# Layer norms between the layers: the inverse root on GpSimd by iteration in place of ScalarE's square root

## The reference

```
def _layernorm(x, axis=-1, eps=1e-05):
    m = jnp.mean(x, axis=axis, keepdims=True)
    v = jnp.var(x, axis=axis, keepdims=True)
    return (x - m) / jnp.sqrt(v + eps)
...
x = _layernorm(x + _L0_attn_ref(x, ...), axis=-1)   # 16 heads, polynomial attention (scores ** 4), causal
x = _layernorm(x + _L0_ffn_ref(x, ...), axis=-1)    # 2 experts, one chosen for each token
x = _layernorm(x + _L1_attn_ref(x, ...), axis=-1)   # 32 heads, softmax attention, causal
x = _layernorm(x + _L1_ffn_ref(x, ...), axis=-1)    # 32 experts, 6 chosen for each token, and a shared one
```

## Time and profile before

| | |
|---|---|
| device time, median of 3 runs | 1570.79 us (1561.16 to 1575.43) |
| span of the profiled execution, first to last instruction | 1555.2 us |
| mean granted clock of TensorE in it | 0.903 |
| instructions | 26255 |
| ACT_TABLE_LOADs | 31, 1283 ns each |
| norms | 16 |

### The profile page before, as it was taken

How to read it: one execution, slowest core, us unless ns; L and a number is a source line. 1 busy time by engine, 2 the same in 40 slices (tenths; PEclk the granted TensorE clock), 3 DMA queues, 4 the chain that set the end, 5 groups by cost and what they waited for, 6 DMA issues and landing times.

```text
span 1555.2 us, 26255 instructions
## 1 busy us (share of the span) xinstructions
PE 1299.0 (84%) x9336; PEld 836.8 (54%) x9336; DVE 1053.5 (68%) x2755; ACT 880.1 (57%) x1250; POOL 673.1 (43%) x834
## 2 busy tenths in 40 slices
PE   6377764776789999689999998889899879899995
PEld 5233352332567877444444554445444445799984
DVE  7767687868543355877888476776887465455675
ACT  2478725778443343337778566676667641466660
POOL 7477334648301103412332741222247626766761
PEclk9589985899899999759999989988889999999999
DMA  2591000012302100000000000000004434677886
GB/s 94 175 362 65 1 1 1 1 41 82 105 32 68 41 15 26 21 1 1 2 1 1 1 1 1 1 2 1 1 31 153 172 144 161 211 210 212 265 263 229
DMA packets 69079, 124.32 MB, mean 80 GB/s; under 512 B 7319, under 2 KB 55127, under 8 KB 67929
## 3 DMA queue, kind: packets, MB, share of 16 engines
q1 hardware_dynamic: 56664, 85.92, 17.2%
q0 software_dynamic: 12288, 36.72, 6.3%
HBM read 60.22 MB, written 62.39 MB: 79 GB/s over the span
## 4 chain that ended last, share of the span: by engine, by line
PE 52%; DVE 26%; ACT 11%; POOL 5%; issue 4%; DMA 2%; SPq 0%; POOLq 0%; DVEq 0%; ACTq 0%
PE psum L2380 9%; PE psum L2275 8%; PE psum L2576 6%; DVE psum L2967 6%; PE psum L2364 6%; PE psum L2475 5%; PE psum L2336 3%; ACT probs L2701 3%; DVE probs L2987 3%; PE psum L2599 3%; PE psum L2496 3%; DVE neg_max L2970 2%; PE psum L351 2%; ACT qt L2618 2%; PE psum L2296 2%
## 5 line engine op out<-in xcount | busy, mean ns | idle before, releaser
L2699 ACT ACTIVATE probs<-psum,exp_shift 128x1024 f32<-128x1024 f32 (+1 forms) x320 | 321.9, 1032 | 137.2 <-PE psum L2364 133.8
L2967 DVE CUSTOM_DVE_ANT_0 psum<-psum,stage 128x512 f32<-128x512 f32 (+3 forms) x512 | 287.1, 621 | 89.0 <-PE psum L2336 88.4
L3552 POOL TENSOR_SCALAR_AFFINE_SELECT probs<-probs 128x512 f32<-128x512 f32 x192 | 139.6, 739 | 410.5 <-ACT probs L2699 308.4
L2364 PE MATMUL psum<-qt,kt 32*128 32x512 f32 (+5 forms) x1152 | 243.4, 456 | 54.7 <-ACT probs L2701 19.4
L2336 PE MATMUL psum<-kt,qt 32*128 32x512 f32 (+3 forms) x768 | 228.8, 467 | 29.9 <-DVE neg_max L2967 21.3
L2364 PEld LDWEIGHTS psum<-qt,kt 32*128 32x128 f32 (+1 forms) x1152 | 108.0, 199 | 214.4 <-issue 84.3
L2987 DVE TENSOR_TENSOR probs<-probs 128x1024 f32<-128x1024 f32 (+1 forms) x136 | 169.6, 1291 | 62.3 <-ACT probs L2701 62.0
L2380 PE MATMUL psum<-probs,v 128*32 128x256 f32 (+3 forms) x2048 | 179.8, 450 | 1.9 <-POOL probs L3552 1.9
L3623 POOL DMA_INDIRECT results<-sp_y,sp_row x128 | 125.7, 982 | 57.2 <-ACT sp_y L2760 28.8
L2336 PEld LDWEIGHTS psum<-kt,qt 32*128 32x128 f32 x768 | 107.5, 204 | 69.7 <-DVE neg_max L2967 42.2
L2701 ACT ACTIVATE probs<-psum 128x1024 f32<-128x1024 f32 (+1 forms) x160 | 140.3, 947 | 5.7 <-PE psum L2364 5.6
(11 more groups left out here) (344 smaller groups left out, 2550.2 us busy)
## 6 DMA issues: line engine op xcount, KB each, us to landing
many_x<-blank SPq DMA_DIRECT2D x2, 10240.0 KB, 50.5
sp_xs<-many_x SPq DMA_DIRECT2D x64, 320.0 KB, 3.7
sp_w<-in_sparse SPq DMA_DIRECT2D x8, 1280.0 KB, 9.8
x_turned<-results SPq DMA_DIRECT2D x8, 768.0 KB, 6.4
sp_back<-results SPq DMA_DIRECT2D x8, 768.0 KB, 9.3
sorted_x<-blank SPq DMA_DIRECT2D x2, 1152.0 KB, 6.5
sorted_y<-y SPq DMA_DIRECT2D x18, 128.0 KB, 1.7
rows<-in_x SPq DMA_DIRECT2D x4, 512.0 KB, 6.8
```

Source lines behind the costliest of these rows:

```text
L2364: inst = pe.matmul(psum[:, base - early:base + QCH - q0], A.kt[rows, k_slot, key * P:(key + 1) * P], A.qt[rows, q_slot, c * QCH + q0 - ear ...
L2699: inst = act.activation(dst, view, ACT.Exp, bias=exp_shift[:, 0:1])
L2967: inst = dve.tensor_tensor_reduce(src, src, causal_bf[:, (4 - cols) * P:4 * P], -1.0, -MASKED, ALU.add, ALU.min, dst)
L3552: pool.affine_select(out=dst, in_=dst, compare_op=ALU.is_ge, fill=0.0, base=0, pattern=[[0, 4], [1, P]], channel_multiplier=-1).then_inc(p ...
```

## The change

The 10 norms that do not stand in the first attention or at the end of the last layer go another way to the inverse root; the other 6 keep the old one (`by_sqrt=True`). In the 10:

- DVE makes the statistics as before; L3023 now multiplies by a constant as well. One more `tensor_scalar` on DVE (`norm_newton`, `ln_rstd<-ln_sd`) makes a first guess of the inverse root: it takes the bits of the number as an integer, halves them and subtracts them from a constant. It stands where `root` stands.
- POOL refines the guess in ten operations on 128x4 numbers, each of which waits for the one before, and then `norm_scale` on POOL runs the four `tensor_scalar` of 128x256 on x.
- ACT has no part in these norms; DVE has no reciprocal and no scaling.
- PE and SP have the same instructions in the same order as before.

```
--- before.py
+++ after.py
@@ -23,6 +23,10 @@
 BANK = 512
 QCH = 512
 EPS = 1e-5
+ROOT_STEPS = ("product", "square", "less", "first", "product 2", "square 2", "less 2", "times 2", "plus 2", "root")
+FIRST_ROOT = 0x5F1FFFF9
+ROOT_A, ROOT_B = 0.703952253, 2.38924456
+ROOT_SCALE = (0.375 * ROOT_A) ** -2
 WEIGHTS_AHEAD = 2
 MANY, WIDTH, SHARED = 32, 96, 192
 GATED = 2 * WIDTH
...
@@ -527,16 +532,23 @@
                     mark(normed, *names[0])
                     mark(normed, *names[1])
                     mark(normed, *names[2])
-                    do("norm_moments", g=g, names=names, ready=ready)
+                    do("norm_moments", g=g, names=names, ready=ready, by_sqrt=by_sqrt)
 
                 def root():
-                    mark(rooted, *names[2])
-                    do("norm_root", g=g, names=names)
+                    if by_sqrt:
+                        mark(rooted, *names[2])
+                        do("norm_root", g=g, names=names)
+                        return
+                    mark(normed, *names[2], "guess")
+                    for what in ROOT_STEPS:
+                        mark(pool_normed, *names[2], what)
+                    do("norm_newton", g=g, names=names)
 
                 def scale():
-                    mark(normed, *names[3])
-                    x_ready[g] = (mark(normed, *names[4]),)
-                    do("norm_scale", g=g, names=names)
+                    if by_sqrt:
+                        mark(normed, *names[3])
+                    x_ready[g] = (mark(normed if by_sqrt else pool_normed, *names[4]),)
+                    do("norm_scale", g=g, names=names, by_sqrt=by_sqrt)
 
                 return [moments, root, scale]
 
@@ -593,7 +605,7 @@
                 norms_due = []
 
                 def norm():
-                    for part in plan_norm(norms_due.pop(0)):
+                    for part in plan_norm(norms_due.pop(0), True):
                         part()
 
                 def x_to_channels(b, c, free):
...
@@ -3008,7 +3020,7 @@
                 dve.tensor_tensor(xs, pair_of_banks(slot).rearrange("p (t n) -> p t n", t=4), xs, ALU.add
                                   ).then_inc(added.by(A.layer, g), 1)
 
-            def norm_moments(g, names, ready):
+            def norm_moments(g, names, ready, by_sqrt):
                 t0, t1 = 4 * g, 4 * g + 4
                 for e in ready:
                     q.wait_ge(*e)
@@ -3020,10 +3032,22 @@
                     inst = dve.bn_aggr(ln_mean_var[:, t, :], ln_stats[:, t, :])
                 inst.then_inc(normed.by(*names[1]), 1)
                 q.wait_ge(normed, *names[1])
-                dve.tensor_scalar(ln_sd[:, t0:t1], ln_mean_var[:, t0:t1, 1], EPS, None, ALU.add
-                                  ).then_inc(normed.by(*names[2]), 1)
-
-            def norm_scale(g, names):
+                if by_sqrt:
+                    dve.tensor_scalar(ln_sd[:, t0:t1], ln_mean_var[:, t0:t1, 1], EPS, None, ALU.add
+                                      ).then_inc(normed.by(*names[2]), 1)
+                else:
+                    dve.tensor_scalar(ln_sd[:, t0:t1], ln_mean_var[:, t0:t1, 1], ROOT_SCALE, ROOT_SCALE * EPS, ALU.mult, ALU.add
+                                      ).then_inc(normed.by(*names[2]), 1)
+
+            def norm_newton(g, names):
+                t0, t1 = 4 * g, 4 * g + 4
+                q.wait_ge(normed, *names[2])
+                dve.tensor_scalar(ln_rstd[:, t0:t1].bitcast(mybir.dt.int32), ln_sd[:, t0:t1].bitcast(mybir.dt.int32),
+                                  -0.5, float(FIRST_ROOT), ALU.mult, ALU.add).then_inc(normed.by(*names[2], "guess"), 1)
+
+            def norm_scale(g, names, by_sqrt):
+                if not by_sqrt:
+                    return
                 t0, t1 = 4 * g, 4 * g + 4
                 q.wait_ge(rooted, *names[2])
                 dve.reciprocal(ln_rstd[:, t0:t1], ln_sd[:, t0:t1]).then_inc(normed.by(*names[3]), 1)
@@ -3544,6 +3568,41 @@
                 pool.tensor_tensor(at_lo, nm, at.bitcast(F32), ALU.subtract).then_inc(pool_cut.by("max", b, g, half), 1)
                 q.wait_ge(pool_cut, "max", b, g, half)
 
+            def norm_newton(g, names):
+                t0, t1 = 4 * g, 4 * g + 4
+                v, y, r, s = ln_sd[:, t0:t1], ln_rstd[:, t0:t1], ln_stats[:, t0:t1, 0], ln_stats[:, t0:t1, 1]
+
+                q.wait_ge(normed, *names[2], "guess")
+                pool.tensor_tensor(r, v, y, ALU.mult).then_inc(pool_normed.by(*names[2], "product"), 1)
+                q.wait_ge(pool_normed, *names[2], "product")
+                pool.tensor_tensor(r, r, y, ALU.mult).then_inc(pool_normed.by(*names[2], "square"), 1)
+                q.wait_ge(pool_normed, *names[2], "square")
+                pool.tensor_scalar(s, r, -1.0, ROOT_B, ALU.mult, ALU.add).then_inc(pool_normed.by(*names[2], "less"), 1)
+                q.wait_ge(pool_normed, *names[2], "less")
+                pool.tensor_tensor(y, s, y, ALU.mult).then_inc(pool_normed.by(*names[2], "first"), 1)
+                q.wait_ge(pool_normed, *names[2], "first")
+                pool.tensor_tensor(r, v, y, ALU.mult).then_inc(pool_normed.by(*names[2], "product 2"), 1)
+                q.wait_ge(pool_normed, *names[2], "product 2")
+                pool.tensor_tensor(r, r, y, ALU.mult).then_inc(pool_normed.by(*names[2], "square 2"), 1)
+                q.wait_ge(pool_normed, *names[2], "square 2")
+                pool.tensor_scalar(s, r, ROOT_A ** 4, -10 / 3 * ROOT_A ** 2, ALU.mult, ALU.add).then_inc(pool_normed.by(*names[2], "less 2"), 1)
+                q.wait_ge(pool_normed, *names[2], "less 2")
+                pool.tensor_tensor(s, s, r, ALU.mult).then_inc(pool_normed.by(*names[2], "times 2"), 1)
+                q.wait_ge(pool_normed, *names[2], "times 2")
+                pool.tensor_scalar(s, s, 5.0, None, ALU.add).then_inc(pool_normed.by(*names[2], "plus 2"), 1)
+                q.wait_ge(pool_normed, *names[2], "plus 2")
+                pool.tensor_tensor(y, s, y, ALU.mult).then_inc(pool_normed.by(*names[2], "root"), 1)
+                q.wait_ge(pool_normed, *names[2], "root")
+
+            def norm_scale(g, names, by_sqrt):
+                if by_sqrt:
+                    return
+                t0, t1 = 4 * g, 4 * g + 4
+                for t in range(t0, t1):
+                    inst = pool.tensor_scalar(x[:, t, :], x[:, t, :], ln_mean_var[:, t, 0:1], ln_rstd[:, t:t + 1],
+                                              ALU.subtract, ALU.mult)
+                inst.then_inc(pool_normed.by(*names[4]), 1)
+
             def mask_weights(A, b, quad, c, step, p_slot, ready):
                 for e in ready:
                     q.wait_ge(*e)
...
```

More of the change, by code:

```diff
@@ L471, in build_program @@
         pool_raised = signal("pool_raised", "POOL")
+        pool_normed = signal("pool_normed", "POOL")
         ident_in, later_in = loading("ident"), loading("later")
@@ L519, in plan_half_to_channels, with plan_norm @@
                 return done
-            def plan_norm(g):
+            def plan_norm(g, by_sqrt=False):
                 names = [("ln", g, next(norm_count), i) for i in range(5)]
@@ L2048, in finish @@
                 def finish(c):
-                    for part in plan_norm(c):
+                    for part in plan_norm(c, True):
                         part()
@@ L2073, in plan_sparse @@
                     if (t, third) == (4, 0):
-                        moments, root, scale = plan_norm(0)
+                        moments, root, scale = plan_norm(0, True)
                         moments()
@@ L3415, in _ @@
                      scores=scores, normalize=normalize, project_out=project_out, norm_moments=norm_moments,
-                     norm_scale=norm_scale, many_setup=many_setup, piece_low=piece_low,
+                     norm_newton=norm_newton, norm_scale=norm_scale, many_setup=many_setup, piece_low=piece_low,
                      sort_by_token=sort_by_token, sort_choose=sort_choose, sort_rank=sort_rank, turn_group=turn_group,
@@ L3627, in _ @@
             walk(dict(attention_setup=attention_setup, bias_setup=bias_setup, project=project, head_scale=head_scale, cut=cut,
[L3628 removed]
+                     cut_max=cut_max, norm_newton=norm_newton, norm_scale=norm_scale, mask_weights=mask_weights, sorted_setup=sorted_setup,
                      piece_low=piece_low, scatter=scatter, gather=gather, many_setup=many_setup,
```

1 line of the change is left out of this document (removed).

## The result

The changed kernel took 1582.74 us (median of 4 runs, 1570.58 to 1593.32) beside 1565.97 us (4 runs, 1561.05 to 1575.43) for the kernel before: a ratio of 1.0119 with a 95% interval of 1.0076 to 1.0161. It is slower by 1.2%. Measured twice more beside experiments, it stood at 1.0115 (1.0075 to 1.0154) and 1.0134 (1.0082 to 1.0185). The forecast was 1569.7 us, within 1% of the kernel before, in a range of 1556 to 1580; the measured time lies above that range.

The account below looks back on a forecast made before the run. No engine is full; PE, busy 84% and half the chain, is bound by its waits around norms. Terms -0.5, 0, +1.7, +6.6, +0.9, -7.6 sum to +1.1 us gained: span 1554.1, plus 15.6 gives 1569.7 us, range 1556 to 1580.

Parts of the forecast that it names:

- 1. norms 2, 3, first expert layer: First expert layer: POOL idle, scaled rows ready at 441.0 and 456.0, PE's turns at 441.49 and 455.00; -0.5 us.
- 3. start of the second attention: Second attention's start: DVE's scaling goes and most of PE's 1.92 us wait with it; +1.7 us (0 to 1.9).
- 4. chunks 0 and 1: Second attention: DVE's maxima no longer held back, 4.65 us, plus 2.0 of clock; +6.6 us (2 to 9.6).
- 5. chunk 2: Second attention: half of PE's 1.83 us wait behind ACT goes, POOL's 5.8 fit before its next mask; +0.9 us.
- 6. chunk 3: Seam to the last layer: norm waits behind POOL's scatters, rows at 1288.7 in place of 1281.11; -7.6 us.
- the clock at chunk 0: Behind PE's wait at chunk 0: granted clock, 0.60 before, rises above 0.9; 1.6 us to be had there.
- the step spacing: POOL's ten dependent operations on 128x4: 0.30 us apart, 3.0 us in all; 2.4 if the overhead guess is too high.
- the table loads: ACT: sixteen table loads of 1.283 us go, 31 become 15, 20.5 us taken from ACT.
- the queue of six scatters at chunk 3: POOL at chunk 3: guess ready at 1279.4, but six scatters stand ahead, the last until 1282.9.
- POOL's scaling: Four scalings of 128x256 on POOL: 0.71 us each, 2.8 together; over 1 us each would show the forecast wrong.
- B: Slower rival: POOL's queue binds at the seam, second attention doesn't pass gains on; 8.9 us lost, 1579.7 us; chance 0.25.
- C: Rival: scaling x on POOL slows DVE where both read SBUF; 2 to 5 us lost; chance 0.05.

Follow-up runs that it names:

- e8: Changed kernel, four subtract-then-multiply scalings of a norm given different operands, constant or for each partition; doesn't compute the layers; ran once, 1592.02 us.
- e10: Changed kernel with other scaling forms on POOL (multiply-then-add with operands for each partition or constants, subtract alone); doesn't compute the layers; ran once, 1637.67 us.
- e11: Changed kernel with POOL's scaling as multiply-then-add and two more small steps, at all ten norms; 1.0065 of the kernel before.
- e1: Changed kernel with the norms of chunks 2 and 3 back on ACT's root and DVE's scaling; 0.9967, repeated 0.9994 of the kernel before.
- e2: Changed kernel with norms 2 and 3 of the first expert layer back on ACT's root and DVE's scaling; 1.0018, repeated 1.0033 of the kernel before.
- e3: Changed kernel with first expert layer's norms 2, 3 and second attention's chunks 2, 3 back on ACT's root and DVE's scaling; 0.9934, repeated 0.9930 of the kernel before.
- e9: Changed kernel with guess, ten steps and scaling all on DVE, no POOL or ACT in the ten norms; 1.0046 of the kernel before.
- e4: Changed kernel with x scaled by DVE again at all ten norms, the ten steps staying on POOL; 1.0056 of the kernel before.

## Why the prediction was wrong

By its own places, with the costs of the table above (us, plus is a gain), and these parted by the windows into PE's waiting and its busy time:

| place | forecast | measured | of it waiting | of it busy time (clock) |
|---|---|---|---|---|
| 1. norms 2, 3, first expert layer | -0.5 | -8.7 | -4.8 | -3.9 |
| 3. start of the second attention | +1.7 | +1.4 | +1.4 | 0.0 |
| 4. chunks 0 and 1 | +6.6 | +6.3 | +4.7 | +1.5 |
| 5. chunk 2 | +0.9 | -6.7 | -3.5 | -3.2 |
| 6. chunk 3 | -7.6 | -9.5 | -9.5 | 0.0 |
| sum | +1.1 | -17.2 | -11.7 | -5.6 |

The forecast is 18.3 us off, nearly all of it at places 1 and 5 (8.2 and 7.6) and 1.9 at place 6. These are readings of one execution of each kernel.

- **What was right.** The waits that go (0.36, none, 2.05 us), with the clock at chunk 0, the step spacing (0.29 us, forecast 0.30), the table loads, and the queue of six scatters at chunk 3. The Trainium skill's 1.4 us of drain at each switch of tables (ScalarE: Activation LUTs, What ACT_TABLE_LOAD costs) would have made place 4 larger; the trace gave 6.3 for it, near the 6.6 that went by the rows.
- **The term that was mis-sized** is POOL's scaling, "because the form is the same and the size can be scaled": 2.8 us for four, measured 4.84. The row scaled from the earlier trace rows is one multiplication; the kernel's operation is a subtraction and a multiplication. I compared the operands and not the operations. e8 and e10 show that the operation is what decides. It costs 2.0 us at each exposed norm, 8 us in all; e11 takes it away and 0.007 of the ratio with it. The prediction had named scalings of over 1 us as a sign of being wrong; they took 1.23.
- **The step that failed** is place 5: "POOL's 5.8 us fit in before its next mask". I looked at what comes next in POOL's queue, and not at what PE wants of it. PE turned these rows 5.67 us after L3023 began (1246.95 to 1252.62) and without a wait, so even at my own price of 5.8 there was no room, and two masks stood ahead in the queue, for 2.6 us. That made 5.36 us of waiting. The gain that I had booked did come, and was larger: PE's waits for ACT behind this turn, 0.74 and 1.83 us, became 0.69 together. But the clock took 3.2 us more. e1 is in line with it: PE has no wait at the turn any more. The seam, this place and chunk 3 together, is worth 0.0084 and 0.0103 of the ratio by e2 against e3.
- **The term put at nothing** is the clock where waits grow: I asked for it only where it could come back. Behind norms 2 and 3 it now falls for some microseconds: PE's lag grows from 4.46 (445.95 against 441.49) to 6.09 at the next statistics (455.89 against 449.80), and from 9.14 to 11.55 behind the second turn, 4 us together, beside 3.2 at chunk 2. It is no chance of one execution: of the profiled executions here, all eleven without ACT's root at these two norms have the second turn at 1.97 us, and all seven with it at 1.09, the time at full clock. Why it fell stays open: in e9 and e11 it fell behind waits of 2.2 us at the first turn, so the longer wait isn't shown to be the cause.
- **The rivals.** B priced place 6 at 8.3 us with 2 more of clock behind it, where 9.5 us of waiting came, and let places 3 and 4 shrink; they did not. Its time was nearest (1579.7), by luck. (Its sum has a -0.6 that no place gives.) Places 1 and 5, where most was lost, stood in none of them. C is not borne out where it can be read: POOL's scalings took the same 4.84 us at the exposed norms, and DVE's maxima at chunk 0 took their usual 0.7 us a piece beside them (0.73 at 1004.24, with POOL's scaling from 1004.14).

## What to carry to other kernels

Moving work to an idle engine pays only where nobody waits for its result next: for each moved step read, in the trace of before, how long after its input the first consumer starts and whether it waits; if that gap is shorter than the new path with its queue, the move costs the difference, and the clock can fall on top. Price an operation from a row with the same operations and not only the same shape. A change made at many places is best judged place by place, by the lag of one engine whose order did not change, and kept only where it gains: chunks 0 and 1 alone gave 0.9962, all ten norms 1.012.

## What was unexpected of the hardware

- On POOL, 128x256 f32 in place: multiply-then-add 0.43 us (constants) and 0.58 (operands for each partition), one subtraction 0.95, subtract-then-multiply 1.07 to 1.23. The same subtract-then-multiply takes DVE 1.38 us for four (in e4, above), 0.35 each, 3.5 times less. The Trainium skill (GPSIMD Engine Reference, Engine selection) calls operations with one tensor input on GpSimd roughly line-rate. With DVE's 0.35 as the measure, multiply-then-add comes near that and subtract-then-multiply doesn't.
- Small dependent operations on 128x4 begin 0.29 us apart on POOL and 0.20 us apart on DVE.
- Where PE's clock is down ahead of a wait, the wait is shorter (2.84 and 5.36 us for the same turn), so the cost of one place differs from execution to execution.
- The clock fell behind a wait of 2.19 us (e11) and stayed up behind one of 3.22 (the kernel before): the length of a wait doesn't tell by itself.
